# Projection weights in homes of their own, and another order of TensorE's work in each attention step

## The reference

```python
q = _fp8_linear_pertensor(ln_out, wq, ...)      # 16 heads of 128, heads normalised
core = _gqa(q, k, v)                            # 8 groups of k and v, two heads each
qx = _fp8_linear_pertensor(ln_out, wqx, ...)    # 16 more heads, on keys and values of the context
xout = _gqa(qx, kx, vx)
catq = _div_clamp_fp8(concatenate([core, xout]), proj_smooth)
out = einsum('bsi,oi->bso', catq, wproj) * (proj_in_scale * proj_w_scale)
```

## Time and profile before

| | us |
|---|---|
| median of 3 runs | 1635.4 |
| profiled execution | 1630.85 |
| its span | 1629.1 |
| TensorE busy (PE) | 1574.2, 97% of the span |
| VectorE busy (DVE) | 1150.1 |
| ScalarE busy (ACT) | 1015.2 |
| GpSimd busy (POOL) | 486.0 |
| mean granted clock of TensorE | 0.995 |

### The profile page before, as it was taken

The page is one execution under the profiler, slowest core; times in us unless marked ns, Lnnn a source line. Parts: engine busy times, 40 slices in busy tenths (PEclk is TensorE's granted clock), DMA queues, the critical chain, the costliest instruction groups (busy, mean ns, idle before and its releaser), DMA issues.

```text
span 1629.1 us, 27708 instructions
## 1 busy us (share of the span) xinstructions
PE 1574.2 (97%) x9392; PEld 1221.4 (75%) x9392; DVE 1150.1 (71%) x2380; ACT 1015.2 (62%) x2855; POOL 486.0 (30%) x515
## 2 busy tenths in 40 slices
PE   7989979999998999999999999999999999999998
PEld 6878766666777767777777777777777777777887
DVE  6358865444997778888888887677777777898322
ACT  4354335553467877877878777777777777875100
POOL 1000222223524333443333443433443343420000
PEclk9999989999999999999999999999999999999999
DMA  8030648885663232364243353121152121110011
GB/s 304 27 109 28 229 167 271 274 270 175 215 228 124 75 135 79 101 237 143 81 136 99 106 199 116 46 77 58 46 201 66 46 109 58 46 39 7 22 38 39
DMA packets 75813, 196.62 MB, mean 121 GB/s; under 512 B 6896, under 2 KB 27376, under 8 KB 69168
## 3 DMA queue, kind: packets, MB, share of 16 engines
q1 hardware_dynamic: 70016, 176.50, 31.6%
q0 software_dynamic: 5680, 18.62, 3.9%
HBM read 147.12 MB, written 47.97 MB: 120 GB/s over the span
## 4 chain that ended last, share of the span: by engine, by line
PE 71%; DVE 8%; ACT 5%; DMA 1%; issue 1%; POOL 1%; SPq 0%; POOLq 0%; ACTq 0%; DVEq 0%
PE bank L2518 9%; PE bank L2517 9%; PE bank L99 8%; PE bank L101 8%; PE bank L100 8%; PE bank L2579 6%; PE bank L2603 5%; PE bank L2568 4%; PE bank L1423 4%; PE bank L1443 4%; PE bank L2589 3%; ACT t_sc L2734 2%; POOL t_rs L2482 1%; PE bank L1403 1%; DVE x_res L1782 1%
## 5 line engine op out<-in xcount | busy, mean ns | idle before, releaser
L2517 PE MATMUL bank<-t_half,t_xh 128*128 128x256 f16 (+1 forms) x1024 | 309.3, 326 | 0.7 <-DVE t_hn L2839 0.7
L2518 PE MATMUL bank<-t_half,t_xh 128*128 128x256 f16 (+1 forms) x1024 | 306.0, 326 | 0.0
L2479 POOL TENSOR_SCALAR t_ve<-t_ss 128x4 f32<-128x4 f32 (+1 forms) x128 | 25.6, 200 | 580.0 <-DVE t_ss L2835 554.4
L2734 ACT ACTIVATE t_sc<-bank,t_mx 128x128 f32<-128x128 f32 x512 | 180.1, 386 | 17.7 <-DVE t_mx L2875 13.1
L2839 DVE TENSOR_TENSOR t_hn<-bank,t_rs 128x256 f32<-128x256 f32 (+1 forms) x256 | 130.0, 549 | 63.4 <-POOL t_rs L2482 63.4
L2482 POOL TENSOR_TENSOR t_rs<-t_ve,t_mhalf 128x4 f32<-128x4 f32 (+1 forms) x128 | 171.0, 1336 | 10.7
L2517 PEld LDWEIGHTS bank<-t_half,t_xh 128*128 128x128 f16 x1024 | 100.3, 98 | 66.7 <-issue 1.4
L2518 PEld LDWEIGHTS bank<-t_half,t_xh 128*128 128x128 f16 x1024 | 100.2, 98 | 66.0
L2772 ACT ACTIVATE t_y<-bank,smooth 128x128 bf16<-128x128 f32 x512 | 139.3, 401 | 2.3 <-DVE t_cq L1303 2.3
L2603 PE MATMUL bank<-t_wp,t_cq 128*128 128x512 f16 x512 | 130.7, 379 | 0.0
L2579 PE MATMUL bank<-t_hT 128*128 128x128 f32 x1024 | 126.2, 276 | 2.7 <-ACT t_hT L2761 2.3
(11 more groups left out here) (355 smaller groups left out, 3878.7 us busy)
## 6 DMA issues: line engine op xcount, KB each, us to landing
t_xh<-xq_scratch SPq DMA_DIRECT2D x64, 512.0 KB, 3.5
t_cr<-in_ctxT_dram SPq DMA_DIRECT2D x64, 256.0 KB, 2.7
t_half<-w_half SPq DMA_DIRECT2D x12, 1024.0 KB, 7.6
y_rows<-s_y SPq DMA_DIRECT2D x39, 256.0 KB, 2.4
e_w<-in_w_units_dram SPq DMA_DIRECT2D x8, 1024.0 KB, 11.8
w_rows<-in_w_qkv_dram SPq DMA_DIRECT2D x8, 1024.0 KB, 5.6
xq_scratch<-z_xs SPq DMA_DIRECT2D x16, 512.0 KB, 3.3
t_slot<-w_plain SPq DMA_DIRECT2D x4, 2048.0 KB, 8.4
```

Source lines behind the costliest of these rows:

```text
L2517: nc.tensor.matmul(out, rows[:, k, kind, :], w[0][:, k, a:b], start=k == 0, stop=False)
L2518: last = nc.tensor.matmul(out, rows[:, k, kind, :], w[1][:, k, a:b], start=False, stop=k == KT - 1)
L2734: last = nc.scalar.activation(sc[:, h, :], b3[4 + part][:, n, :], ACT.Exp, bias=mx[:, h:h + 1], accum_out=sm[:, h:h + 1])
```

## The change

TensorE's step gets the order: turned probabilities, six output products, turned heads, attended values, two output products, scores (`OUT_FIRST = 6`). The projection weights get a tile for each quarter, `wp[q]`, in the upper 8 KB of the slot that holds the quarter's float16 query weights; ScalarE's wait for `pj_ps` goes, and the four copies go to two steps (i % 16 of 1 and 2), two in each: one before `values`, one before `scaled_out`. `xT_lo1` of the dense block moves to the place of the old `wp` (122). The pieces of the last rows are spread over steps 1 to 7, and they are rounded and stored with i-1 in (2, 3, 5, 6) instead of (1, 3, 4, 5). On VectorE the late weights' `means`, first `centre_heads` and second `lo_segs` come after `sums_a` instead of before `normalise_b`.

```diff
--- before.py
+++ after.py
@@ -1907,8 +1907,8 @@
                                 ("expert", kv, kv + 8, D)):
             self.raw[name] = at("raw_" + name, lo, [P, KT, n])
             self.w[name] = [at(f"{name}_hi", hi, [P, KT, n], F32R), at(f"{name}_lo", lo, [P, KT, n], F32R)]
-        self.hi, self.lo = ([at(f"xT_{n}{c}", kb + 8 * i, [P, KT, CW], F32R) for c, kb in enumerate((kvx, wq, wqx, 64))]
-                            for i, n in enumerate(("hi", "lo")))
+        self.hi = [at(f"xT_hi{c}", kb, [P, KT, CW], F32R) for c, kb in enumerate((kvx, wq, wqx, 64))]
+        self.lo = [at(f"xT_lo{c}", kb, [P, KT, CW], F32R) for c, kb in enumerate((kvx + 8, 122, wqx + 8, 72))]
         even = at("xn0", 151, [P, J, D])
         self.xn = [even, at("xn1", wqx + 8, [P, J, D]), even, at("xn3", 160, [P, J, D])]
         self.h_hi, self.h_lo = (at("h_" + n, 96 + 8 * i, [P, KT, CW], F32R) for i, n in enumerate(("hi", "lo")))
@@ -2302,7 +2302,6 @@
     vv_lo = [sb(f"vv_lo{i}", 160 + 2 * i, [P, 2 * QG, P], F32R) for i in range(2)]
     y = sb("y", 116, [P, 2, QH * P], BF16)
     cq = [sb(f"cq{i}", 118 + 2 * i, [P, KH, P], F16) for i in range(2)]
-    wp = sb("wp", 122, [P, 8, D], F16)
     c_hi = sb("c_hi", 164, [P, KT, P], F32R)
     c_lo = sb("c_lo", 166, [P, KT, P], F32R)
     cr0 = sb("cr0", 112, [P, KT, P])
@@ -2323,6 +2322,7 @@
     b3 = [bank[i][:].rearrange("p (h n) -> p h n", n=P) for i in range(8)]
     M = Q * B
     FIRST, LOOPS = 3, 4
+    OUT_FIRST = 6
 
     KV, KVX, WQ_, WQX, SPARE = range(5)
     homes = [[1, 2, 4, 0, 3]]
@@ -2330,8 +2330,10 @@
         kv, kvx, wq, wqx, spare = homes[-1]
         homes.append([spare, kv, kvx, wq, wqx])
 
-    LAST_ROWS = (1, 3, 4, 5)
-    ROW_PIECES = {1: range(0, 3), 2: range(3, 4), 3: range(4, 6), 4: range(6, 9), 5: range(9, 12), 6: range(12, 16)}
+    wp = [sb(f"wp{q}", SLOTS[homes[q][WQ_]] + 8, [P, 8, D], F16) for q in range(Q)]
+    LAST_ROWS = (2, 3, 5, 6)
+    ROW_PIECES = {1: range(0, 1), 2: range(1, 2), 3: range(2, 5), 4: range(5, 8), 5: range(8, 11), 6: range(11, 14),
+                  7: range(14, 16)}
     de = Dense(nc, env, ctx, mem, homes[Q - 1], late, wp_in, a_ps, e_in, x_in, mhalf)
 
     def side(part):
@@ -2598,9 +2600,10 @@
                                           vv_lo[par][:, v, :], pT[:, h:h + 2, :], pT_lo[:, h:h + 2, :], True, True)
                 last.then_inc(pv_ps, 1)
 
-        def output_heads(par, heads):
+        def output_heads(m, par, quarter, heads):
             for h in heads:
-                last = nc.tensor.matmul(bank[5][:], cq[par][:, h, :], wp[:, h, :], start=h == 0, stop=h == KH - 1)
+                last = nc.tensor.matmul(bank[5][:], cq[par][:, h, :], wp[quarter_of(m, quarter)][:, h, :], start=h == 0,
+                                        stop=h == KH - 1)
             return last
 
         def output_begin(m, par, read, quarter):
@@ -2610,14 +2613,14 @@
             pe.wait_ge(ex_in, read)
             if later(m, 1):
                 pe.wait_ge(x_in, m)
-            output_heads(par, range(QH))
-
-        def output_end(m, par):
-            output_heads(par, range(QH, KH)).then_inc(pj_ps, 1)
+            output_heads(m, par, quarter, range(OUT_FIRST))
+
+        def output_end(m, par, quarter):
+            output_heads(m, par, quarter, range(OUT_FIRST, KH)).then_inc(pj_ps, 1)
 
         def output(m, par, read, quarter):
             output_begin(m, par, read, quarter)
-            output_end(m, par)
+            output_end(m, par, quarter)
 
         def step(i, par, quarter):
             if has(i + 1):
@@ -2629,10 +2632,10 @@
                 output_begin(i - 3, 1 - par, min(i, M) * 2 if isinstance(i, int) else i * 2, quarter)
             if has(i):
                 turn(i)
-            if has(i - 3):
-                output_end(i - 3, 1 - par)
             if has(i - 1):
                 attend(i - 1, 1 - par)
+            if has(i - 3):
+                output_end(i - 3, 1 - par, quarter)
             if has(i):
                 scores(i)
             if has(i + 1):
@@ -2672,12 +2675,11 @@
     def scalar(act):
         def wproj(quarter, part):
             i, a = divmod(part, 2)
-            if quarter and part == 0:
-                act.wait_ge(pj_ps, quarter * B)
             if part == 0:
                 act.wait_ge(wraw_in, quarter * 16 + 16)
             raw = slots32[homes[quarter][SPARE]]
-            last = nc.scalar.activation(wp[:, 4 * i + 2 * a:4 * i + 2 * a + 2, :], raw[:, i, 2 * a:2 * a + 2, :], ACT.Copy)
+            last = nc.scalar.activation(wp[quarter][:, 4 * i + 2 * a:4 * i + 2 * a + 2, :], raw[:, i, 2 * a:2 * a + 2, :],
+                                        ACT.Copy)
             if a:
                 last.then_inc(wp_in, 1)
 
@@ -2688,8 +2690,8 @@
                 sh.scaled(act, C - 1, k, (v,))
 
         def wproj_part(i, part):
-            if isinstance(i, int) and i % B == 2 and i < M:
-                wproj(i // B, part)
+            if isinstance(i, int) and i % B in (1, 2) and i < M and part % 2 == 0:
+                wproj(i // B, 2 * (i % B - 1) + part // 2)
 
         def squares_a(m):
             if later(m, 1):
@@ -2915,17 +2917,17 @@
                 de.normalise(dve, 0, range(2))
             if number(i) == M - 2:
                 de.normalise(dve, 0, range(2, J))
-            if opened is not None:
-                late.means(dve, opened)
-                late.centre_heads(dve, opened, 0)
-            if split is not None:
-                late.lo_segs(dve, split, late.SEGS[2:4])
             if has(i):
                 normalise_b(i)
             if has(i - 1):
                 probs_low(i - 1)
             if has(i + 1):
                 sums_a(i + 1)
+            if opened is not None:
+                late.means(dve, opened)
+                late.centre_heads(dve, opened, 0)
+            if split is not None:
+                late.lo_segs(dve, split, late.SEGS[2:4])
             if not later(i, 1):
                 sh.rounded(dve, C - 2, KT - 1)
             if has(i - 2):
```

## The result

The changed kernel takes 1655.5 us (median of 4 runs, 1654.2 to 1658.2) against 1636.6 of the kernel before on the same chip: ratio 1.013, 95% interval 1.0113 to 1.0146. It is slower by some 19 us on the medians; 18.3 were forecast, to 1653.7.

A forecast was written before the change was run, and what follows sets the result against it. The prediction took TensorE's own stream to bound the attention steps. Its terms, +15.9, +1.9, -1.8, -3.6 and +5.9, summed to +18.3 us, giving a median of 1653.7 us, range 1644 to 1662.

The forecast's parts named there:

- Part 1: TensorE's order: scores' second half waits for the residual, ending 0.95 to 1.01 after scores start (S); 0.27 a step, +15.9 us.
- The tie at hT: ScalarE's hT ends at 1176.65, the scores' first weight load begins at 1176.71; at most 0.05 us lost.
- Part 2: VectorE's late work behind sums_a makes the residual end near S + 1.2 in 8 block-opening steps; +1.9 us.
- Part 3: Row pieces and rounding of the last chunk in new places: turned heads wait less in late steps; -1.8 us.
- part 5: First late-weight load, issued only after the last rounding, loses its cover and VectorE's sums wait; +5.9 us.
- Rival 1: Late-weight load lands under the maxima, so sums wait for nothing; 1647.8 us, chance 0.17.
- Rival 2: Granted clock falls to half rate after TensorE stands still for the late load, costing 2 to 4 us; 1657, chance 0.18.
- Part 4: Homes for projection weights, with ScalarE's copies split over two steps, shorten the quarters' first steps; -3.6 us.
- Rivals 3 and 4: Residual's round trip hides: with the load landing in time, 1630 us, chance 0.08; with it exposed, 1636, chance 0.05.

The follow-up runs named there:

- e3: Changed kernel with the last two output products between the two halves of the attended values; 1644.5 us, ratio 1.0033 to the kernel before.
- e10: Changed kernel with the residual taken over the first 256 of its 512 columns only; one run, 1639.6 us.
- e1: Changed kernel with TensorE's old order alone put back (four output products, turned heads, four output products, attended values, scores); 1643.1 us, ratio 1.0036.
- e6: Changed kernel with the loops of the third and fourth quarter written out; one run, 1650.9 us.
- e13: Changed kernel with all eight output products before the turned heads, last rows rounded in steps 3 to 6, late work back before normalise_b; one run, 1647.0 us.
- e5: Changed kernel with VectorE's late work back before normalise_b; 1648.0 us, ratio 1.0082 to the kernel before.
- e4: Changed kernel with LAST_ROWS and ROW_PIECES as before, so late weights load a step earlier; 1654.1 us, ratio 1.0099 to the kernel before.
- e2: Kernel before with the new order of TensorE alone; 1652.6 us, ratio 1.0092.
- e7: Kernel before with the projection weights' homes and their copies in two steps alone; 1631.1 us, ratio 0.9968.

## Why the prediction was right, point by point

- **Part 1, the round trip**: right in mechanism and size. Residual from S + 0.21 to S + 0.96 (0.20 to 0.26 and 0.95 to 1.01 predicted), 0.27 to 0.29 us lost in plain steps. e3 (distance), e10 (VectorE's share) and e1 (order) each remove it. What I missed is 1.3 us in the loops, where by all signs a register instruction, hidden before, came onto the trip (e6).
- **The tie at hT**: right; the first weight load of the scores is released by hT, and S moves by 0.03 us at most (5.33 to 5.36 into the step). e13 shows what lies one step beyond.
- **Part 2, late work on VectorE**: the term that was mis-sized: 1.9 predicted, 5.7 to 6.0 measured (e5: 4.7 in seven opening steps, 1.0 in steps 7 and 8). Its own rows give more than its S + 1.2: the residual starts at S - 0.65 in the earlier trace rows, and 1.4 us of work in front of it makes it end near S + 1.5; S + 1.2 needs `normalise_b` at 0.57 into the step, the 0.84 of the earlier trace rows less the 0.27 by which the step grows. Measured are 1.05 and S + 1.62. An opening step comes right after a step in which VectorE has low parts to make, and I had treated each kind of step by itself. VectorE from the step before on:

```profile
712.57 0.75 DVE L2900 SCALAR_TENSOR_TENSOR x_res<-bank,coef,x_res 128x512 f32<-128x512 f32 x1 [0.38 <-PE bank L2605]
713.24 0.68 DVE L274 TENSOR_TENSOR l_lo_plain<-l_rows,l_hi_plain 128x512 fp32r<-128x512 f32 x1
...
715.23 1.27 DVE L2877 TENSOR_REDUCE t_mx<-bank 128x4 f32<-128x512 f32 x2
```

  From the residual to the next maxima it is 2.66 us here and 2.05 in an ordinary step of the changed kernel (1211.21 to 1213.26). Before the change VectorE had a wait of 0.88 us for `values_low` behind the residual, in which a low part could hide; the later residual has used it up.
- **Part 3 with part 5**: steps 1 to 8 cost 5.6 us more than before; my terms for them give some 6 (-1.8, +5.9, six shares of 0.27 of part 1 and one of 0.24 of part 2). The transfer alone costs 6.4 (e4). Part of this fit is luck. The load went out 11.6 us into its step, where I had put 10.2, since that step was itself late (rounding had made the step before end late); and its data was read 6.2 us after issue, where 7.1 was taken. The two misses nearly cancel. Rival 1 is out.
- **Rival 2**: its clock came, its price did not. TensorE stood still 3.51 us up to 625.75, and the granted clock was 0.66 on average in 625 to 630. The Trainium skill (TensorE: Matmul & The Clock Gate, "Why this matters for your kernels") warns that a gap between bursts brings half rate; this trace agrees. What it cost can be read from step 7, at a granted clock of 1.00, and step 8:

```profile
608.14 1.29 DVE L2841 TENSOR_TENSOR t_hn<-bank,t_rs 128x512 f32<-128x512 f32 x2 [1.28 <-POOL t_rs L2484]
...
612.05 2.23 PE L2581 MATMUL bank<-t_hT 128*128 128x128 f32 x16
...
629.78 1.29 DVE L2841 TENSOR_TENSOR t_hn<-bank,t_rs 128x512 f32<-128x512 f32 x2 [1.28 <-POOL t_rs L2484]
...
633.70 1.05 PE L2581 MATMUL bank<-t_hT 128*128 128x128 f32 x8
```

  The scores start 3.91 and 3.92 us after `normalise_b`: TensorE had to wait for VectorE's heads anyway, and the slow stretch lay in that time. So the 2 to 4 us of rival 2 are nil here; they were 1.2 in step 19 of e2, where the slow stretch came once VectorE's heads were there.
- **Part 4, homes**: -3.6 predicted for quarters 2 to 4, -5.0 measured in e7, the like measure. The -4.0 of the changed kernel holds six round trips of 0.27 as well, so the homes gave some 5.6 there. The gain was put too low by 1.4 to 2.0.
- **Rivals 3 and 4** needed a round trip that hides; plain steps of 15.38 rule them out.

The sum was 3.0 too low over the steps: 21.3 us against 18.3. Late work (4) and loops (1.3) were put too low, and the homes' gain, put too low as well, takes some 2 of that back. The medians differ by 18.9, nearer to the forecast than the steps or the spans of the two profiled executions (1629.1 and 1652.5): that nearness is spread between executions and not accuracy.

## What to carry to other kernels

When two users of a PSUM bank are moved close together, price the whole trip: last product, the reader's wake-up, the reader's instruction, the wake-up of TensorE; here 1.07 us from the end of the last product's stream to the next weight load, where the first half of the scores covers 0.78. The order in which two products moved by 1.4 us cost 12 us of 1636 (e1) because they were the last writers. And look for what became the last arrival in a neighbouring step: a slack that exists in an ordinary step may have been spent by the step before. A wait that costs nothing in one order of work, like ScalarE's for `pj_ps`, has to be priced again in the other (e2).

## What the runs showed of the hardware

- A wait of TensorE of some 0.3 us need not show as idle time of its products: their busy time rose from 296.2 to 298.6 of 300 us while the steps grew from 15.10 to 15.38. It shows as 0.20 us in the weight loads' row and in the distance between starts.
- The residual over 256 instead of 512 columns takes 0.48 instead of 0.75 us. From these two an estimate: some 0.2 of the 0.75 us do not depend on the columns.
- In a loop, a register instruction (57 to 81 ns) runs ahead of VectorE's residual, and the residual starts at S + 0.33 instead of S + 0.21 when VectorE has been waiting; written out, it starts at S + 0.20.
- The granted clock fell behind shown waits of TensorE of 3.51 us (changed kernel), 2.22 us (e2) and 2.29 us (e4, step 2), and stayed at 1.00 behind one of 2.61 us in the kernel before; the length of the wait that is shown does not settle it alone. Its price depends on what follows: nil in the changed kernel, 1.2 us in e2, 0.7 us in e4.
